# Reordering the set-up of an attention and quantised-projection kernel, and moving its clock-keeping matmuls

## What is computed

```python
xn = (x - mean(x)) / sqrt(var(x) + 1e-5)
qkv = xn @ w_qkv.T + b_qkv                       # q, k, v: [B, 16 heads, 512, 16]
att = q @ k.T / sqrt(16) + position_bias         # cos/sin of (i - j), and a constant per head
att = softmax(where(causal, att, -inf))
a = (att @ v) @ w_proj.T + b_proj
xq = float8_e4m3(bf16(xn) / s_in); kq = float8_e4m3(kernel / s_k)
f = bf16((xq @ kq) * (s_in * s_k)) + bias
return x + a + f
```

## Time and profile before

| what | value |
|---|---|
| median of 3 executions | 786.15 us (785.88 to 789.09) |
| the profiled execution | 785.88 us, of which 784.1 us are the profile's span |
| mean granted TensorE clock | 0.983 of full speed |
| TensorE busy | 743.5 us, 95% |
| VectorE busy | 633.5 us, 81% |
| ScalarE busy | 580.4 us, 74% |
| GpSimd busy | 531.5 us, 68% |

### The profile page before, as it was taken

The page is one execution under the profiler, slowest core; times in us unless marked ns, Lnnn a source line. Parts: engine busy times, 40 slices in busy tenths (PEclk is TensorE's granted clock), DMA queues, the critical chain, the costliest instruction groups (busy, mean ns, idle before and its releaser), DMA issues.

```text
span 784.1 us, 23212 instructions
## 1 busy us (share of the span) xinstructions
PE 743.5 (95%) x6328; PEld 500.8 (64%) x6330; DVE 633.5 (81%) x2395; ACT 580.4 (74%) x1262; POOL 531.5 (68%) x525
## 2 busy tenths in 40 slices
PE   7889999999999999999999999999999999999983
PEld 4556567666766666676666766666676667666552
DVE  5798788888879888888988888898888888888602
ACT  5357878778777878778787878878787787886660
POOL 8244766686776768676776867677666867757560
PEclk9989999999999999999999999999999999999987
DMA  5603352434344343533444253344524333444102
GB/s 177 242 31 123 120 176 106 170 116 146 127 149 171 142 132 116 177 121 125 171 149 139 108 187 132 119 148 153 173 99 170 120 141 133 150 145 148 49 18 88
DMA packets 55612, 106.07 MB, mean 135 GB/s; under 512 B 10528, under 2 KB 30496, under 8 KB 55584
## 3 DMA queue, kind: packets, MB, share of 16 engines
q1 hardware_dynamic: 54440, 105.06, 37.8%
q10 hardware_dynamic: 1144, 0.67, 0.3%
HBM read 18.68 MB, written 8.91 MB: 35 GB/s over the span
## 4 chain that ended last, share of the span: by engine, by line
PE 75%; DVE 8%; ACT 7%; issue 5%; DMA 3%; DVEq 1%; SPq 1%; ACTq 1%; POOL 1%; POOLq 0%
PE misc_a L672 15%; PE misc_a L556 13%; PE misc_b L556 10%; PE scoreT_b L646 9%; PE scoreT_a L646 5%; PE score_c L623 4%; PE score_a L623 3%; PE misc_b L672 3%; PE misc_b L607 3%; ACT qk_parts L851 2%; PE scoreT_b L649 2%; DVE row_max L1041 2%; DVE qk_parts L1029 1%; ACT probs L963 1%; PE scoreT_a L649 1%
## 5 line engine op out<-in xcount | busy, mean ns | idle before, releaser
L1241 POOL TENSOR_SCALAR_AFFINE_SELECT probs<-probs 128x512 f32<-128x512 f32 x256 | 160.0, 635 | 193.1 <-ACT probs L963 189.8
L1041 DVE CUSTOM_DVE_ANT_0 score_b<-score_b,causal_mask_q 128x384 f32<-128x384 f32 (+3 forms) x321 | 162.5, 523 | 91.2 <-PE score_b L623 91.1
L1041 DVE CUSTOM_DVE_ANT_0 score_a<-score_a,causal_mask_q 128x512 f32<-128x512 f32 x319 | 174.7, 564 | 2.0 <-PE score_a L623 1.8
L1041 DVE CUSTOM_DVE_ANT_0 score_c<-score_c,causal_mask_q 128x256 f32<-128x256 f32 (+3 forms) x384 | 172.0, 475 | 3.3 <-PE score_c L623 3.2
L963 ACT ACTIVATE probs<-scoreT_b 128x384 f32<-128x384 f32 (+1 forms) x256 | 132.3, 517 | 46.7 <-PE scoreT_b L649 22.7
L963 ACT ACTIVATE probs<-scoreT_a 128x512 f32<-128x512 f32 (+1 forms) x256 | 143.3, 560 | 8.7 <-PE scoreT_a L649 7.6
L1041 DVE DVE_READ_ACCUMULATOR2_ANT row_max<- 128x1 f32 x1024 | 143.1, 140 | 0.0
L963 ACT ACTIVATE probs<-scoreT_c 128x384 f32<-128x384 f32 (+1 forms) x256 | 133.8, 523 | 0.5
L672 PE MATMUL misc_a<-probs,v_ones 128*32 128x128 f32 (+3 forms) x1536 | 129.1, 439 | 4.5 <-POOL v_ones L1268 1.7
L646 PE MATMUL scoreT_b<-stacks 64*128 64x384 f32 (+3 forms) x320 | 121.1, 398 | 1.8 <-ACT probs L963 1.7
L623 PE MATMUL score_b<-stacks 64*128 64x384 f32 (+3 forms) x321 | 117.2, 397 | 1.0 <-DVE row_max L1041 0.6
(11 more groups left out here) (250 smaller groups left out, 1929.6 us busy)
## 6 DMA issues: line engine op xcount, KB each, us to landing
stacks<-qk_parts SPq DMA_DIRECT2D x128, 512.0 KB, 3.7
x_ring<-in_L_attn_x SPq DMA_DIRECT2D x16, 512.0 KB, 3.6
attn<-out_T SPq DMA_DIRECT2D x63, 128.0 KB, 2.6
xn<-recips SPq DMA_DIRECT2D x31, 256.0 KB
out<-x_ring SPq DMA_DIRECT2D x15, 512.0 KB, 3.0
stacks<-neg_max_T SPq DMA_DIRECT2D x128, 4.0 KB
low_features<-neg_max_T SPq DMA_DIRECT2D x126, 4.0 KB
low_features<-probs SPq DMA_DIRECT2D x8, 128.0 KB, 4.5
```

The lines of the kernel that those rows point to most:

```text
L1041: last = V.tensor_tensor_reduce(bank, bank, CMQ[:, T - w:T], 1.0, LEAST, ALU.add, ALU.max, MX[:, g % 2, 8 * h + 4 + qt:8 * h + 5 + qt])
L1241: last = GP.affine_select(out=d, in_=d, compare_op=ALU.is_ge, fill=0.0, base=0, pattern=[[0, HU], [1, P]], channel_multiplier=-1)
```

## The change

It changes the set-up part and the first body, on two engines; GpSimd, ScalarE and SyncE keep their order. On VectorE the wait for the small inputs and the three scale instructions go ahead of `T_lo`; the statistics of sequence 1 go ahead of `QK_lo` 0; the lo parts of the output weights, the last `QK_lo` and the guard steps of sequence 0 go ahead of the chunk maxima, the guard steps out of the first body; the bias sum goes ahead of the quantiser's weight steps. On TensorE four of the eight clock-keeping matmuls before the products are gone; the bias projection moves from after chunk 10 to after chunk 7, and its waits to before chunk 0; each chunk of group 1 but one is followed by a clock-keeping matmul.

```diff
@@ -75,7 +75,7 @@
 
 INVERT_AT, LAST_INVERT_AT = (0, 8), (3, 8)
 STATS_AT, AGGR_AT = [(1, 3), (1, 3), (1, 6), (1, 6)], (1, 7)
-MAGIC_AT, FIRST_MAGIC_AT = [(2, 1), (2, 2), (2, 3)], [(0, 1), (0, 3), (0, 4)]
+MAGIC_AT = [(2, 1), (2, 2), (2, 3)]
 
 
 FIRST_CHUNKS = [0, 1, 4, 5, 8, 9, 2, 3, 6, 7, 10, 11]
@@ -704,7 +704,7 @@
             pe.wait_ge(head_made, 3)
             pe.wait_ge(feat_raw, 48)
             mm(STB[1][:, 0:2], HEAD[:, :], POS[:, 0:1].broadcast_to([P, 2]), start=True, stop=True).then_inc(csum_ready, 1)
-            warm(8, STB[2])
+            warm(4, STB[2])
             pe.wait_ge(setup_lo, 2)
             for m in range(2):
                 pe.wait_ge(xb_ready, m + 1)
@@ -723,12 +723,11 @@
                 last.then_inc(setup_T, 1)
             for m in (2, 3):
                 job_QK(0, m)
-            pe.wait_ge(setup_lo, 3)
+            pe.wait_ge(setup_lo, 5)
+            pe.wait_ge(bq_scaled, 1)
 
             def project_bias():
 
-                pe.wait_ge(setup_lo, 5)
-                pe.wait_ge(bq_scaled, 1)
                 for ct in range(CT):
                     for i, w in enumerate((PH, PL)):
                         last = mm(STB[0][:, 0:C], BQ[:, 4 + ct:5 + ct].broadcast_to([P, P]), w[:, ct, :].bitcast(F32),
@@ -742,7 +741,7 @@
                 in_turn(scores(0, 0, c, n))
                 if n in (2, 4):
                     job_V(0, n // 2 - 1)
-                elif n == 10:
+                elif n == 7:
                     project_bias()
                 else:
                     warm(1, STB[2])
@@ -753,6 +752,8 @@
                 if c == 2:
                     for ct in range(CT):
                         job_T(1, ct)
+                else:
+                    warm(1, STB[2])
             pe.wait_ge(consts_made, 4)
             pe.wait_ge(bp_made, 1)
 
@@ -1101,38 +1102,40 @@
                                        in1=WH[:, ct, 0:C].bitcast(F32), op0=ALU.mult, op1=ALU.subtract)
                 V.tensor_tensor(WL[:, ct, C:2 * C], SB_[ct][:, C:2 * C], WH[:, ct, C:2 * C].bitcast(F32),
                                 ALU.subtract).then_inc(setup_lo, 1)
-            for ct in range(CT):
-                T_lo(0, ct)
             dve.wait_ge(small_loaded, 16 * 7)
             then(V.reciprocal(SC[:, 4:5], SC[:, 1:2]))
             then(V.reciprocal(SC[:, 2:3], SC[:, 0:1]))
             then(V.tensor_tensor(SC[:, 3:4], SC[:, 0:1], SC[:, 1:2], ALU.mult))
+            for ct in range(CT):
+                T_lo(0, ct)
+            for t in range(TT):
+                stats(1, t)
+            aggregate(1)
             QK_lo(0, 0)
             QK_lo(0, 1)
             dve.wait_ge(setup_hi, 3)
             V.tensor_tensor(WL[:, :, 2 * C:3 * C], SB_[2][:, :].rearrange("p (a c) -> p a c", c=C),
                             WH[:, :, 2 * C:3 * C].bitcast(F32), ALU.subtract).then_inc(setup_lo, 1)
+            for ct in range(CT):
+                dve.wait_ge(setup_hi, 4 + ct)
+                V.tensor_tensor(PL[:, ct, :], STB[ct][:, 0:C], PH[:, ct, :].bitcast(F32), ALU.subtract) \
+                    .then_inc(setup_lo, 1)
             QK_lo(0, 2)
-            for t in range(TT):
-                stats(1, t)
-            aggregate(1)
+            quant_magic(0, 0)
+            quant_magic(0, 1)
+            QK_lo(0, 3)
+            quant_magic(0, 2)
             dve.wait_ge(ident_steps, 5)
             dve.wait_ge(consts_made, 1)
             for n, c in enumerate(FIRST_CHUNKS):
                 chunk_max(0, 0, c, n)
-                if n == 3:
-                    QK_lo(0, 3)
-                if n in (5, 6):
-                    dve.wait_ge(setup_hi, n - 1)
-                    V.tensor_tensor(PL[:, n - 5, :], STB[n - 5][:, 0:C], PH[:, n - 5, :].bitcast(F32), ALU.subtract) \
-                        .then_inc(setup_lo, 1)
+            dve.wait_ge(bp_ready, 1)
+            V.tensor_tensor(BP[:, :], STB[0][:, 0:C], BP[:, :], ALU.add).then_inc(bp_made, 1)
             dve.wait_ge(kq_step, 3)
             V.tensor_scalar(ke.bitcast(I32), kt.bitcast(I32), 0x7F800000, None, ALU.bitwise_and).then_inc(kq_step, 1)
             dve.wait_ge(kq_step, 4)
             V.scalar_tensor_tensor(out=km, in0=ke, scalar=E4_LEAST, in1=km, op0=ALU.max, op1=ALU.mult) \
                 .then_inc(kq_step, 1)
-            dve.wait_ge(bp_ready, 1)
-            V.tensor_tensor(BP[:, :], STB[0][:, 0:C], BP[:, :], ALU.add).then_inc(bp_made, 1)
             for c in range(CHUNKS):
                 chunk_max(0, 1, c)
                 if c in (6, 8):
@@ -1165,9 +1168,6 @@
                                 stats(b + 2, t)
                             if (g, k) == AGGR_AT:
                                 aggregate(b + 2)
-                        if first:
-                            for part in due(FIRST_MAGIC_AT, g, k):
-                                quant_magic(0, part)
                         if not last:
                             for part in due(MAGIC_AT, g, k):
                                 quant_magic(b + 1, part)
```

## The result

The changed kernel is slower, by more than the prediction's range of 784.5 to 790.3 us allowed. Four executions have a median of 795.55 us (794.39 to 799.81) against 786.01 us (784.02 to 789.09) for the kernel before: ratio 1.0128, 95% interval 1.0077 to 1.0179. The profiled execution took 793.11 us, of which 791.4 are the span, so it is 7.2 us above the one of before; the mean granted clock fell from 0.983 to 0.972.

A forecast was written before the change was run, and what follows sets the result against it. TensorE, busy for 95% of the span, was taken as the bound, with start shifts carried to the end. Terms +2.7 + 1.3 - 0.74 + 1.35 - 1.5 - 1.67 = +1.4 us gave 787.3, stated as 787.6; range 784.5 to 790.3.

The forecast's parts named there:

- term of +1.35 us: Group 1: eleven added clock-keeping matmuls make TensorE set the pace, +1.35 us, bounds 0 and +1.5.
- the step after it: First body step: full clock kept and three guard steps gone from VectorE, -1.5 us.
- Rival (d): Low clock outlasts the start's products and TensorE falls again in group 1: 790.5 us, chance 0.13.
- The start: Before group 0: scales ahead of low parts, +2.7 us, and four clock-keeping matmuls fewer, +1.3 us.
- 2.7: Start, VectorE: low part waits for small inputs and scales, starting at 15.9 instead of 13.20, +2.7 us.
- (a): Start: the clock holds, or the tiny scale instruction is not held; 786.3 us, with both 785.5; chance 0.13.
- (c): Start: small inputs are there before 14.5, so it does not move; -2.6 alone, 783.6 us; chance 0.04.
- +1.3 for the low clock: Start: after a 3.8 us TensorE pause the twelve products begin at 1.2 GHz, +1.3 us within 0 to 2.0.
- Group 0: Last query/key low part ahead of the chunk maxima removes TensorE's wait at 27.90, -0.74 us.
- Values-beside-ones: First body: TensorE's wait for GpSimd's values-beside-ones goes, as guard steps are done earlier, -1.67 us.
- signs that the prediction named as right: Low part about 15.9, TensorE idle nearly 4 us, first pair 3 to 5 us later, full-clock body step, no values-beside-ones wait.
- those it named as wrong: Low part at 13.2, full clock 16 to 20 us with products in 3.3 us, or TensorE ahead in group 1.

The follow-up runs named there:

- projection in slot 10: Changed kernel with the bias projection after chunk 10 of group 0 again, group-1 matmuls kept: 787.47 us, ratio 0.9982 to the kernel before.
- pause filled: Changed kernel, projection still after chunk 7, with three clock-keeping matmuls added in the pause ahead of group 1: 787.50 us, ratio 1.0013 to the kernel before.
- the second profile: Profile of the changed kernel measured once more, unaltered, beside the kernel before on another batch's chip: 793.86 us, ratio 1.0097.
- theory C: No single run: the follow-up theory that moving the dense projection away leaves thin work ahead of group 1's pause, so the clock falls there in nearly every execution.
- the repeat of slot 10: Changed kernel with the bias projection after chunk 10 once more, on another chip: 789.57 us, ratio 1.0025 to the kernel before.

## Why the prediction was wrong

**Group 1 is the step that failed**, in two sentences of it. The term of +1.35 us was worked out at the full clock, and the step after it said "With TensorE kept at work the fall at 43.5 should not come". At the full clock the two together were right to 0.13 us. With the pitches that the prediction took, TensorE needs 2 x 0.74 + 0.37 + 1.02 + 0.74 + 8 x 0.69 = 9.1 us for the group, and 9.24 (projection in slot 10) and 9.25 (pause filled) were measured. The prediction's boundary between group 1 and the body step is on VectorE and the table's on TensorE, so the two are compared together: forecast 1.35 - 1.5 = -0.15 us; from the group's first chunk to the next sequence's first product it is 51.09 - 37.60 = 13.49 before, 13.47 with the pause filled (38.26 to 51.73), and 20.20 in the changed kernel, **+6.7**. The fall did come, 0.9 us into the group instead of 6.0. The pitch at the low clock, 1.16 us, is more than VectorE's 0.52 to 0.65: the group took 15.03 us, 5.8 more than at the full clock.

The error behind it is that TensorE's clock was taken as the result of added work, more matmuls and therefore no fall. The runs show two parts. What stands ahead changes how often the clock falls at the group's start: the changed kernel has the eight matmuls of the projection, 1.9 us in a row, away from the pause, and what is left there is chunks of 64 rows, single matmuls and 0.93 us of nothing; moving the projection back or filling the pause removes most or all of the loss. And what stands in the group goes with how long it stays down: with single matmuls between chunks it did not come back before the body's own work, though TensorE's records are gapless. The matmuls thus turned a low stretch of 6.8 us that VectorE hid into one of 17 to 20 us on the critical path.

**Rival (d)** named this mechanism and this group, and got 0.13; its 790.5 us is 5 short. Two of its sizes were off. It let the fall come where it had come before, behind the transposes, and so priced four matmuls at 0.17 us each (+0.7) and a body step as before (+1.5). It came ahead of nearly all eleven pairs, and each pair costs 0.46 us more, the chunk's part of it too. The remark against it, "twice as many columns go through", is the same error as above: in the seven profiles with a low stretch more columns went through and the clock stayed down for longer. What the earlier trace rows could have said is that from 44 to 46 us TensorE was busy for 1.94 of 2 us at a granted clock of 0.50: a nearly full row at the low clock was there to be read, and it should have made "kept at work" worth less.

**The start**: forecast +4.0 in two terms (2.7 + 1.3), measured +2.9 in one profile of the changed kernel and +1.2 in the other. Of the 2.7 only 1.4 came: the small inputs landed 0.5 us earlier, at 14.0, and being earlier the tiny multiplication ran ahead of GpSimd's instruction rather than beside it (0.16 for 0.95 us). That is part of rivals (a) and (c). "At 14.5 and not before" was read from one execution, and the landings of 13.1 to 15.3 us show how much of this term is luck. (The prediction's text on (c) has -2.6 alone as 783.6 us; that figure is 787.6 - 2.7 - 1.3, with the low clock of the products gone too. Alone it is 785.0.) The +1.3 for the low clock was 1.5 where the clock fell behind the pause of 2.59 us, and nothing in the second profile, whose pause was 1.82; there the clock fell in group 0 and cost as much. Of the eight profiles with four matmuls at the start and the late products, three fell behind pauses of 2.59 to 2.74 us and five held, four of them with 1.82 to 2.29 and one with 2.58. The Trainium skill (GPSIMD Engine Reference, Specifications) has VectorE instructions with two SBUF inputs contend for the interface that GpSimd shares; the trace agrees: in the four profiles in which the multiplication starts while GpSimd's instruction runs it takes 0.22 to 0.95 us and ends within 0.02 us of that one's end, and in the other thirteen it takes 0.16 or 0.17.

**Group 0**: forecast -0.74, measured -0.80 (and +0.67 in the second profile, with its low stretch there). **Values-beside-ones**: forecast -1.67, measured -1.8, with no wait left. So all without group 1 and the body step was forecast at 4.0 - 0.74 - 1.67 = +1.6 us and is 2.9 - 0.8 - 1.8 = +0.3; the two in the middle were forecast at -0.15 and are +6.7. The error of the total is theirs. Of the signs that the prediction named as right, the full clock in the first body step did not show, and the late low part, the idle time and the late first pair came smaller (14.59, 2.59 and 2.9 us for 15.9, nearly 4 and 3 to 5). Of those it named as wrong, the full clock from 16 to 20 us showed in the second profile.

**From 7.2 to 9.5 us.** The profiled execution is the fastest of the changed kernel's five; the others have 47.6 to 57.5 low us to its 44.3. With the price below, 0.3 us for each low one, the middle two (47.6 and 50.9) account for some 1.5 us of the remaining 2.3, an estimate.

**What stays open.** Why the kernel before with the same matmuls falls only in about half of its executions, whether its projection stands in slot 10 or in slot 7, is not settled: the changed kernel also makes other things earlier on VectorE, and none of the runs separates those. That theory C missed three of its forecasts (the kernel before with the projection in slot 7, the filled pause without group-1 matmuls, the repeat of slot 10) says that the work in front of the pause is not the whole condition. Nor is the start's part settled: with the old start the ratio is 1.0048 for 1.0097 to 1.0128, and the products' own delay of about 1 us explains only part. The Trainium skill (TensorE: Matmul & The Clock Gate, What's actually happening) has the throttled state as the default from which activity releases; the rows here agree, and add that a TensorE without gaps in its records need not be active enough. What in the alternating pairs falls short, the 64 rows or something else, no run here shows.

## What to carry to other kernels

A clock-keeping matmul is insurance only where TensorE has time to spare at either clock: work out the pitch of the pair at 1.2 GHz (here 1.16 us) beside that of the engine that sets the pace (0.52 to 0.65), and if it is longer, a fall at its start turns the insurance into the bound. Put such matmuls in the pause in front of a thin stretch (here three of them in 0.93 us cost nothing and returned 6 to 8 us) rather than between the instructions of the stretch. And read the granted clock row by row beside the busy share: in the changed kernel the products of the start got the clock back while they ran, and the pairs of group 1, with the same busy share of 2.00 in 2 us, did not. A full busy share does not promise the full clock.

## What the runs showed of the hardware

The spread of one program's times, which I had taken as noise, goes mostly with the time that TensorE spends at 1.2 GHz. The 27 executions of the kernel before in the last batch run from 783.7 to 789.6 us, with 20 to 38 low us each, and a straight line through them is 777.7 us + 0.30 us for each low one; through those of the first batch it is 777.6 + 0.31. The three fastest executions of all, 780.27, 780.40 and 780.84 us, had 11, 25 and 25 low us. In the profile of before 20.5 of some 27 low us lie in the last 51 us of the span, where the program is the same in all kernels, and from profile to profile this late part goes from 13.7 to 30.8 us.

By these lines half the clock costs only about a third of the time that it lasts. In the changed group 1, where TensorE sets the pace, it was 5.8 us for the 14.2 low us inside the group, some 0.4; that the rest is hidden by other engines' pace is likely and was not tested.

A low stretch can outlast a good deal of unbroken work: up to 20.5 us here with TensorE recorded as busy throughout. Nor did other operands shorten it in the one profile that has them: with the constant mask the stretch in group 1 was 17.1 to 20.5 us, with real weights 20.5.

The one-column multiplication of the scales, where it starts while GpSimd's tensor_tensor of 1.04 us runs, ends with it. In four profiles it took 0.95, 0.79, 0.66 and 0.22 us, each time what was left of GpSimd's instruction; in the other thirteen it took 0.16 or 0.17.
